# The last of four blocks of du times B, made by VectorE between its scans instead of by TensorE with a scaled identity

## The reference

```python
dt = jax.nn.softplus(dt_low @ W_dt + b_dt)
A = -jnp.exp(A_log)

def step(h, inp):
    dt_t, B_t, C_t, u_t = inp
    dA = jnp.exp(dt_t[:, :, None] * A)
    h = dA * h + (dt_t * u_t)[:, :, None] * B_t[:, None, :]
    y = jnp.einsum('bdn,bn->bd', h, C_t)
    return (h, y)
```

## Time and profile before

| what | value |
|---|---|
| median of three runs | 1761.86 us (1759.6 to 1762.43) |
| the profiled execution, its own time | 1759.05 us |
| its span in the profile | 1757.3 us |
| TensorE, VectorE, ScalarE, GpSimd busy | 88%, 49%, 43%, 28% |
| mean granted clock of TensorE | 0.933 |
| scan, first to last product of GpSimd | 338.1 to 667.1 us |

### The profile page before, as it was taken

One profiled execution on the slowest core, in us unless ns is written; L12 is line 12 of the kernel. 1 busy time (PEld: TensorE's weight loads), 2 busy tenths in 40 slices (PEclk: granted clock), 3 DMA queues, 4 the chain that ended last, 5 costly groups with the idle time before them and its releaser, 6 DMA issues.

```text
span 1757.3 us, 19033 instructions
## 1 busy us (share of the span) xinstructions
PE 1542.7 (88%) x7116; PEld 873.3 (50%) x7116; DVE 857.8 (49%) x885; ACT 763.5 (43%) x1172; POOL 489.7 (28%) x139
## 2 busy tenths in 40 slices
PE   5787897698989896789998588888899999999998
PEld 3665333597979793554443122222354444444443
DVE  4994657699888895564430776666210000000000
ACT  1232475799898881123323066656522112221221
POOL 0997200398888881400222200000000000000000
PEclk7899898799999998679999599999989999999999
DMA  3000003122222113210100931211000000000000
GB/s 145 16 10 1 10 40 146 48 85 97 97 96 73 49 49 135 93 26 11 54 36 36 213 134 53 55 36 36 1 0 0 0 12 0 12 0 0 12 0 12
DMA packets 32080, 84.88 MB, mean 48 GB/s; under 512 B 5091, under 2 KB 21569, under 8 KB 29569
## 3 DMA queue, kind: packets, MB, share of 16 engines
q1 hardware_dynamic: 30081, 82.21, 13.9%
q10 hardware_dynamic: 1920, 1.57, 0.7%
HBM read 66.79 MB, written 16.91 MB: 48 GB/s over the span
## 4 chain that ended last, share of the span: by engine, by line
PE 56%; POOL 16%; DVE 10%; issue 8%; ACT 4%; DVEq 4%; DMA 1%; ACTq 0%; SPq 0%; POOLq 0%
POOL arena L2112 15%; PE ps L1258 13%; PE ps L1273 13%; PE ps L1130 4%; PE ps L1017 3%; DVE mxs L1985 3%; PE ps L1170 2%; DVE arena L1669 2%; PE ps L1110 2%; DVEq L1668 2%; PE ps L754 2%; PE ps L1039 2%; PE ps L967 1%; ACT arena L1594 1%; PE ps L745 1%
## 5 line engine op out<-in xcount | busy, mean ns | idle before, releaser
L2112 POOL TENSOR_TENSOR arena<-arena 128x2048 f32<-128x2048 f32 x64 | 289.9, 4555 | 166.9 <-DVE arena L1768 166.8
L1768 DVE TENSOR_TENSOR_SCAN arena<-arena,ps 128x1024 f32<-128x1024 f32 x128 | 283.8, 2271 | 46.3 <-issue 23.2
L1258 PE MATMUL ps<-arena 128*128 128x512 f32 x512 | 241.9, 598 | 0.0
L1636 ACT ACTIVATE arena<-ps,arena 128x512 f32<-128x512 f32 x128 | 87.9, 687 | 348.9 <-PE ps L1258 348.9
L1273 PE MATMUL ps<-arena 128*128 128x512 f32 x512 | 239.3, 592 | 0.0
L1985 DVE TENSOR_REDUCE mxs<-ps 128x1 f32<-128x512 f32 x256 | 162.0, 684 | 71.7 <-PE ps L1110 70.2
L1459 ACT ACTIVATE arena<-arena,mam 128x511 f32<-128x511 f32 x256 | 165.3, 708 | 33.6 <-DVE arena L1768 33.6
L1594 ACT ACTIVATE arena<-ps,rho 128x1024 f32<-128x1024 f32 x128 | 140.5, 1111 | 88.5 <-PE ps L1170 88.3
L2072 DVE SCALAR_TENSOR_TENSOR arena<-ps,b2s,arena 128x512 f32<-128x512 f32 x8 | 5.6, 747 | 334.4 <-PE ps L1273 334.4
L1258 PEld LDWEIGHTS ps<-arena 128*128 128x128 f32 x512 | 97.9, 192 | 121.6 <-issue 121.6
L1273 PEld LDWEIGHTS ps<-arena 128*128 128x128 f32 x512 | 97.3, 190 | 122.5 <-issue 122.5
(11 more groups left out here) (300 smaller groups left out, 1887.4 us busy)
## 6 DMA issues: line engine op xcount, KB each, us to landing
arena<-bc_scratch SPq DMA_DIRECT2D x32, 512.0 KB, 3.6
batch_scratch<-arena SPq DMA_DIRECT2D x2, 3072.0 KB, 9.0
arena<-batch_scratch SPq DMA_DIRECT2D x6, 1024.0 KB, 7.9
arena<-q_scratch SPq DMA_DIRECT2D x96, 64.0 KB, 2.1
arena<-in_cond SPq DMA_DIRECT2D x1, 5019.5 KB, 24.1
arena<-k_scratch SPq DMA_DIRECT2D x72, 64.0 KB, 2.1
mam<-in_ids SPq DMA_DIRECT2D x4, 768.0 KB, 7.4
q_scratch<-arena SPq DMA_DIRECT2D x4, 768.0 KB, 3.3
```

What stands on the lines that cost most here:

```text
L1258: last = pe.matmul(ps[:, 2 + f % 4, :], w1[:, c, f * P:(f + 1) * P], y4[:, b if isinstance(b, int) else bass.ds(b, 1), c, :], start=(c == ...
L1768: dve.tensor_tensor_scan(half, view(decay[:, (2 * k + h) % 3], [[1, 2 * S]]), view(ps[:, FEED + 2 * h, :], [[1, 2 * S]]), 0.0, ALU.mult, A ...
L2112: pool.tensor_tensor(state[:, k % SLOTS], state[:, k % SLOTS], view(c_rows[:, j % 2, k % G, :], [[0, M], [1, S]]), ALU.mult).then_inc(s_hc, 1)
```

## The change

The last time block of du times B is no longer a product with a scaled identity. VectorE makes it by a tensor_scalar of 128x512 from `duT` to `dub` (both in SBUF), with the column of B as a scalar for each partition, for step k + 1 between the two scans of step k. TensorE transposes it as it does the other three blocks. ScalarE no longer scales the identity. A new semaphore tells TensorE that the block is there. Besides, four semaphores of the gate of the expert stage become two that count further; each wait stays behind the same instruction.

```diff
             def feed(k, h):
                 if h == 0:
                     pe.wait_ge(s_dub, k + 1)
+                    pe.wait_ge(s_dub3, k + 1)
                 if k:
                     pe.wait_ge(s_scan, 2 * k - 1 + h)
                 for m in (2 * h, 2 * h + 1):
-                    for t in range(TILES - 1):
-                        pe.transpose(ps[:, FEED + m, t * P:(t + 1) * P], dub[:, k % 2, t, m * P:(m + 1) * P], ident)
-                    last = pe.matmul(ps[:, FEED + m, LAST:S], duT[k // NS % 2][:, TILES - 1, m * P:(m + 1) * P],
-                                     dub[:, k % 2, TILES - 1, 0:P], start=True, stop=True)
+                    for t in range(TILES):
+                        last = pe.transpose(ps[:, FEED + m, t * P:(t + 1) * P], dub[:, k % 2, t, m * P:(m + 1) * P], ident)
                 last.then_inc(s_dbu, 1)
...
                 for t in range(TILES - 1):
-                    act.activation(dub[:, k % 2, t, :], duT[b % 2][:, t, :], ACT.Copy, scale=bt[:, b, t, n:n + 1])
-                last = act.activation(dub[:, k % 2, TILES - 1, 0:P], ident, ACT.Copy, scale=bt[:, b, TILES - 1, n:n + 1])
+                    last = act.activation(dub[:, k % 2, t, :], duT[b % 2][:, t, :], ACT.Copy, scale=bt[:, b, t, n:n + 1])
                 last.then_inc(s_dub, 1)
...
+            def times_b(k):
+                b, n = divmod(k, NS)
+                if b >= 2 and n == 0:
+                    dve.wait_ge(s_back_dt, 32 * (b - 1))
+                if k >= 2:
+                    dve.wait_ge(s_dbu, 2 * k - 2)
+                dve.tensor_scalar(dub[:, k % 2, TILES - 1, :], duT[b % 2][:, TILES - 1, :], bt[:, b, TILES - 1, n:n + 1],
+                                  None, ALU.mult).then_inc(s_dub3, 1)
+
+            dve.wait_ge(s_duT, 2 * B)
+            dve.wait_ge(s_bt, B)
+            times_b(0)
             for k in range(B * NS):
                 b, n = divmod(k, NS)
                 scan(k, 0)
+                if k + 1 < B * NS:
+                    times_b(k + 1)
                 if b and n in (4, 5):
                     residual(b - 1, n - 4)
                 scan(k, 1)
```

More of the change, by code:

```diff
@@ L230, in program @@
         FEED = 4
-        LAST = (TILES - 1) * P
         head_at = B * M * S * 2 + B * C * S
@@ L286, in program @@
         s_dub = sem("du_times_b")
+        s_dub3 = sem("du_times_b_last_block")
         s_dbu = sem("du_times_b_turned")
@@ L475, in program @@
         s_gate_mm = sem("gate_products")
[L476 to L479, removed]
+        s_gate_v = sem("gate_parts_by_vector")
+        s_gate_a = sem("gate_parts_by_scalar")
         s_ng = sem("gate_factor")
@@ L1623, in _ @@
                 last.then_inc(s_y4, 1)
-            act.wait_ge(s_gate_sq, 1)
+            act.wait_ge(s_gate_v, 1)
             act.activation(gs[:, 1, :], gs[:, 0, :], ACT.Ln, scale=1.0 / E, bias=eps32[:, 0:1])
             act.drain()
-            act.activation(gs[:, 1, :], gs[:, 1, :], ACT.Exp, scale=-0.5).then_inc(s_gate_r, 1)
-            act.wait_ge(s_gate_d, 1)
-            act.activation(lg[:, :, :], lg[:, :, :], ACT.Exp, scale=2.0).then_inc(s_gate_e, 1)
+            act.activation(gs[:, 1, :], gs[:, 1, :], ACT.Exp, scale=-0.5).then_inc(s_gate_a, 1)
+            act.wait_ge(s_gate_v, 2)
+            act.activation(lg[:, :, :], lg[:, :, :], ACT.Exp, scale=2.0).then_inc(s_gate_a, 1)
             act.preload_act_table_set("gelu_and_others")
@@ L2042, in _ @@
             dve.drain()
-            dve.tensor_reduce(gs[:, 0, :], lg2[:, :, :], AX, ALU.add).then_inc(s_gate_sq, 1)
+            dve.tensor_reduce(gs[:, 0, :], lg2[:, :, :], AX, ALU.add).then_inc(s_gate_v, 1)
             dve.drain()
@@ L2046, in _ @@
             dve.drain()
-            dve.wait_ge(s_gate_r, 1)
+            dve.wait_ge(s_gate_a, 1)
             dve.tensor_tensor(lg2[:, :, :], lg2[:, :, :], view(gs[:, 1, :], [[1, B * TILES], [0, E]]), ALU.mult)
@@ L2052, in _ @@
             dve.tensor_tensor(lg[:, :, :], lg2[:, :, :], view(gs[:, 2, :], [[1, B * TILES], [0, E]]),
-                              ALU.subtract).then_inc(s_gate_d, 1)
-            dve.wait_ge(s_gate_e, 1)
+                              ALU.subtract).then_inc(s_gate_v, 1)
+            dve.wait_ge(s_gate_a, 2)
             dve.tensor_reduce(gs[:, 0, :], lg[:, :, :], AX, ALU.add)
```

## The result

The changed kernel took 1892.76 us (median of four runs, 1892.5 to 1893.34) against 1762.14 us before (four runs, 1759.6 to 1764.6): 1.0742 times as long, 95% interval 1.0723 to 1.076. The forecast was 1892 us in 1880 to 1912.

What follows compares the result with a forecast made beforehand. VectorE's scans bind 45 of 63 periods, TensorE 18. 62 x 7.17 = 444.5, + 3.6 + 2.1 + 9.1 gives 459.3 us against 329.0; with 0.4 more, + 130.7 on the 1761.86 median makes 1892 us, range 1880 to 1912.

Steps and rivals of the forecast that it cites:

- The blocked product: Between a step's scans, VectorE's tensor_scalar waits until GpSimd's product ends; regular steps become 7.17 us; chance 0.88.
- The last term: Time from the end of GpSimd's product to the tensor_scalar's end: 0.34 us, bounds 0.05 to 0.69.
- The sum: Stretch from GpSimd's first product in the scan to its last: 459.3 us after the change, against 329.0 before.
- the residuals: Two residuals behind the tensor_scalar, n = 4 and 5 of three batches, add 6 x 0.6 = 3.6 us.
- the end 9.0 for 9.1: The last step has no tensor_scalar, so two GpSimd products follow each other: 4.50 + 4.56 = 9.1 us.
- the three steps n = 6: Steps n = 6 of three batches, after the late residual, are 0.7 us longer each: 2.1 us.
- the scan starts at E + 11.0 less 0.2: Start of n = 6's scan, E being a second scan's end: residual at E + 5.6, then 5.5 us, shorter feed.
- Rival 1: No block between tensor_scalar and GpSimd's product in the scan: VectorE pays 18.9 us, TensorE returns 7.9; 1772 us; chance 0.04.
- Rival 2: TensorE's relief in 18 periods wins 7.9 us, VectorE's product almost free: 1754 us; faster or no change 0.02 together.
- Rival 3: TensorE's clock falls in the scan; heavy steps n = 3 to 6 add 24 us: 1916 us; chance 0.06.
- the main case: VectorE's tensor_scalar in the scan is blocked until GpSimd's product ends: 1892 us; chance 0.88.
- fully blocks: Skill's rule for two-port VectorE instructions against GpSimd: the later waits, whole 0.48 us following GpSimd's end; forecast 1901 us.

Runs made afterwards that it cites:

- experiment 1: Kernel before plus a 128x384 VectorE product that nothing reads: 1889.15 us; separately, changed kernel with VectorE's product for the first two steps only: 1753.07 us.
- experiment 3: Changed kernel with GpSimd's product cut to three of four chunks: 1831.17 us; separately, with VectorE's product on half the channels (128x256): 1882.21 us.
- experiment 5: Changed kernel with the residuals of n = 4 and 5 ahead of VectorE's product instead of behind it: 1883.73 us.
- experiment 2: Changed kernel with the same product at the same place as a scalar_tensor_tensor whose second operand comes from PSUM and is dropped: 1792.6 us.
- the relief alone: Changed kernel with VectorE's product made for the first two steps only, leaving the savings of TensorE and ScalarE: 1753.07 us.
- experiment 4: Changed kernel with the same product behind the second scan of a step, made two steps ahead: 1770.6 us.
- last run of experiment 6: Kernel before with VectorE's product in one-SBUF-input form for n = 4 to 9 of the last three batches, and residuals ahead of the first scan: 1749.46 us.
- The version of experiment 6 with VectorE's product for n = 4 to 9: Kernel before with VectorE's one-SBUF-input product for n = 4 to 9 of the last three batches, behind the residual: 1754.23 us.
- the last two runs of experiment 6: Kernel before with residuals ahead of the first scan: alone 1754.79 us; with VectorE's one-SBUF-input product for n = 4 to 9 too, 1749.46 us.

## Why the prediction was right, point by point

**The blocked product.** Confirmed step by step: the record 2.80 us, the end 0.28 us behind GpSimd's (forecast 0.34), the start of GpSimd 0.08 behind the scan, the regular step 7.10 us (forecast 7.17). Experiments 1 to 4 show the mechanism apart from the number. The gap in the evidence, that no row before showed a tensor_scalar against GpSimd's tensor_tensor, was bridged rightly by the cast and the memset. The last term, the time from GpSimd's end to the product's, came out smaller than by L1821: 0.28 us for 0.34. It goes with the width, 0.28 us for 512 columns, 0.22 for 384 (experiment 1) and 0.15 for 256 (experiment 3), so that the rest of the product's own 0.46 us lies under the wait.

**The sum.** 62 steps were 0.07 us shorter each, 4.3 us in all; the residuals 3.7 us for 3.6; the end 9.0 for 9.1; the three steps n = 6 took 8.6 us over the regular step for the 2.1 of the forecast. 440.2 + 3.7 + 8.6 + 9.0 = 461.5, measured 461.64, forecast 459.3. So two errors of 4.3 and 6.5 us partly cancelled, and the stretch came out 2.3 us longer than forecast, and it began 0.4 us later. That the total met all the same is luck: the forecast added 2.8 us, by which the profiled execution of the kernel before was under its median, and in the changed kernel the profiled execution (1892.5) is only 0.3 us under the median. The hit of 1892.76 against 1892 is better than the terms were.

**The term that was mis-sized** is "the scan starts at E + 11.0 less 0.2". It took the D term, the sum and the feed at the 5.5 us of the kernel before, with TensorE at 2.4 GHz. TensorE now paused for 4.40 us for the residual, its clock was at 1.2 GHz when it went on or just after, and the same work, worked out at 5.3 us, took 494.09 - (486.94 + 0.06) = 7.1 us in the first of the three, and 8.1 and 6.8 in the others. That the late residual is on the path is shown by experiment 5; why the clock falls there isn't.

**Rival 1**, no block, was refuted for this instruction and is what experiment 2 shows for another one: 5.01 us steps. **Rival 2**, TensorE's relief: it is there (1762.61 - 1753.07 = 9.5 us in experiment 1 for the relief alone, with an interval of some 3 us), though by the steps it is 6.8 us where the clock holds and not 7.9, since n = 4 and n = 6 give only about half of the 0.44. The price that it allowed, 0.18 us a step, is undercut by no form tried in all 64 steps: 0.35 is the least. **Rival 3**, the clock, was half right: the granted clock of the stage fell to 0.88 and to 0.83 in plain steps, and those held at 7.10 us as worked out; what it cost lay in n = 6 alone, about 6 us instead of 24. The forecast gave it 0.06 as a case of its own. It came together with the main case, and would have been better put as a term of it.

**The range** held the time. The prediction's rule from the Trainium skill ("SBUF — State Buffer", "Who interferes with whom") was right on the exclusion and on the order of issue deciding who is blocked (experiment 4 shows both orders with one instruction). Taken for a price, the Trainium skill's "fully blocks" would have given 0.48 behind GpSimd's end; the trace has 0.28.

## What to carry to other kernels

The price of a fast VectorE instruction isn't a property of the instruction alone. Beside GpSimd's products a tensor_scalar of 0.46 us from SBUF to SBUF cost as long as the product in progress still had to run. So look at what GpSimd is doing at that place before you price such an instruction, and try the form with an operand in PSUM, or a place just ahead of GpSimd's release. Move work off an engine only in the steps where that engine ends the wait. And an instruction that feeds another engine belongs in front of one that may block, even where it delays it.

## What was not expected

- The place of one instruction on its queue was worth 122 us of 1893 (experiment 4).
- In the blocked order a part of the loser's own time is hidden: its end is 0.28 us behind the winner's for 512 columns, of 0.46 us that it takes alone. GpSimd as the loser pays 0.17 us for a product that ends 0.4 us after it is released.
- The versions with shorter feeds had a lower clock at one place. With the relief alone, TensorE's pause for the residual at n = 5 grew from 1.92 to 2.31 us in the first batch of three, and the granted clock there was 0.82 in two of the three, for 9.6 us from first scan to first scan instead of 8.1. TensorE's timeline before, of the relief alone, and windows of the relief alone (the columns of the earlier trace rows):

```profile
437.48 0.39 PE L824 MATMUL ps<-arena 128*128 128x512 bf16 x1 [1.92 <-DVE xT L1760]
```

```profile
436.98 0.63 PE L824 MATMUL ps<-diag,arena 128*128 128x128 f32 x2 [2.31 <-DVE xT L1756]
```

```profile
433.70:443.30 9.60, 7.29 (x52) 7.21 (x54) 5.04 (x4) 5.87 (x10) 8.94 (x2) 0.82 0.01 2
518.00:526.10 8.10, 5.97 (x52) 5.90 (x54) 5.12 (x4) 5.93 (x10) 7.46 (x2) 1.00 0.00 2
```

The kernel before held 1.00 in all three batches of its one profiled execution. It is tempting to blame the longer pause, and the expectation of the last run of experiment 6 does. But the version of experiment 6 with VectorE's product for n = 4 to 9 pauses for 1.90 us at the same place, no longer than the kernel before, and has 0.82 there in two of three batches too:

```profile
520.20:529.90 9.70, 7.64 (x52) 7.46 (x54) 5.75 (x6) 5.84 (x9) 8.45 (x2) 0.82 0.01 3
```

The version of experiment 4 pauses for 2.29 us and has 0.82 in all three. So the length of the pause alone doesn't decide, and what does stays open. With the residuals ahead of the first scan (the last two runs of experiment 6) TensorE doesn't pause there at all, and the clock held 1.00 in all six batches.
